# Delta-rule stage of a four-layer decoder: the triangular inverses of two steps in flight, their rounds issued in pairs, the inverse put together by ScalarE

## The reference, cut to what matters

```python
mixed = silu(causal_conv4(x @ Wqkv.T));  q, k, v = split(mixed)
z, b, a = x @ Wz.T, x @ Wb.T, x @ Wa.T
beta = sigmoid(b);  g = -exp(A_log) * softplus(a + dt_bias)
q, k = l2norm(q) / sqrt(128), l2norm(k)
for t in range(64):
    state = state * exp(g[t])
    delta = (v[t] - state.T @ k[t]) * beta[t]
    state = state + outer(k[t], delta)
    out[t] = state.T @ q[t]
y = (rmsnorm(out) * norm_w * silu(z)) @ Wout.T
```

## Time and profile before

| | |
|---|---|
| runs of before | 4779.5, 4787.9, 4791.57 us; median 4787.9 us |
| profiled execution: its span, the only time given for it | 4786.8 us |
| PE, DVE, ACT, POOL busy over the span | 86%, 68%, 44%, 32% |
| projection 0 of step 0 starts | at 2238.71 us of the span |
| last residual addition of the stage ends | at 4132.07 us of the span |

### The profile page before, as it was taken

How to read it: one execution, slowest core, us unless ns; L and a number is a source line. 1 busy time by engine, 2 the same in 40 slices (tenths; PEclk the granted TensorE clock), 3 DMA queues, 4 the chain that set the end, 5 groups by cost and what they waited for, 6 DMA issues and landing times. The chain is left out here.

```text
span 4786.8 us, 142961 instructions
## 1 busy us (share of the span) xinstructions
PE 4133.9 (86%) x62052; PEld 2708.2 (57%) x62052; DVE 3251.6 (68%) x6025; ACT 2096.0 (44%) x3703; POOL 1514.4 (32%) x1605
## 2 busy tenths in 40 slices
PE   7627886677767887997999999999999999789999
PEld 6415654323325664444677777777777777455555
DVE  7897745788897886754677777777777777531111
ACT  3446533544444554323555555555555555221111
POOL 1001200298893220000443334433344433112222
PEclk9869997888898998998999999999999999789999
DMA  1000000133341001001000000000010000041111
GB/s 34 19 27 11 2 12 20 67 121 119 120 141 37 2 2 34 20 1 40 15 21 21 21 24 21 21 21 21 21 26 23 21 17 4 8 128 53 49 53 44
DMA packets 72967, 175.11 MB, mean 37 GB/s; under 512 B 14578, under 2 KB 27892, under 8 KB 69748
## 3 DMA queue, kind: packets, MB, share of 16 engines
q1 hardware_dynamic: 72340, 165.96, 11.1%
HBM read 163.04 MB, written 2.88 MB: 35 GB/s over the span
## 5 line engine op out<-in xcount | busy, mean ns | idle before, releaser
L1721 POOL TENSOR_TENSOR ssm_ub<-ssm_dtu,ssm_bcn 128x512 f32<-128x512 f32 x256 | 324.4, 1293 | 299.5 <-DMA ssm_bcn<-ssm_bct 297.1
L2485 POOL TENSOR_TENSOR dn_eb<-dn_ee,dn_cc 128x512 f32<-128x512 f32 x64 | 66.7, 1042 | 1034.2 <-DVE dn_cc L2599 1034.2
L3030 DVE TENSOR_TENSOR moe_hh<-moe_si,moe_pu 128x512 f32<-128x512 f32 x104 | 71.4, 688 | 450.5 <-PE moe_pu L2919 444.3
L2527 DVE SCALAR_TENSOR_TENSOR core_XN<-dn_bA,dn_w,core_XN 128x504 f32<-128x504 f32 (+2 forms) x384 | 280.6, 731 | 24.9 <-ACT core_XN L2361 4.9
L1620 ACT ACTIVATE ssm_da<-core_XN,ssm_al 128x504 f32<-128x504 f32 x240 | 163.2, 683 | 253.5 <-DVE ssm_ph L1788 169.0
L2982 POOL TENSOR_TENSOR moe_hw<-moe_hh,moe_cb 128x512 f32<-128x512 f32 x100 | 126.6, 1266 | 444.2 <-DVE moe_hh L3030 392.7
L2963 ACT ACTIVATE moe_si<-moe_pg 128x512 f32<-128x512 f32 x104 | 62.1, 597 | 467.7 <-PE moe_pg L2919 467.7
L2191 PE MATMUL dn_bA<-core_XT,dn_w 128*128 128x512 f32 x512 | 258.8, 629 | 9.0 <-ACTq L2453 4.4
L1608 PE MATMUL ssm_py<-ssm_hc,core_ident 128*128 128x512 f32 x352 | 200.6, 675 | 61.7 <-DVE ssm_hc L1792 31.2
L2325 PE MATMUL dn_po<-dn_wo,dn_cT 128*128 128x256 f32 x1024 | 242.1, 390 | 2.6 <-issue 1.4
L1788 DVE TENSOR_TENSOR_SCAN ssm_ph<-ssm_da,ssm_ub 128x512 f32<-128x512 f32 x168 | 204.9, 1220 | 29.3 <-POOL ssm_ub L1721 17.1
(11 more groups left out here) (498 smaller groups left out, 10429.9 us busy)
## 6 DMA issues: line engine op xcount, KB each, us to landing
ssm_bcn<-ssm_bct SPq DMA_DIRECT2D x128, 512.0 KB, 3.6
dn_cb<-dn_cum SPq DMA_DIRECT2D x32, 512.0 KB, 5.0
dn_w<-in_dn_w SPq DMA_DIRECT2D x32, 388.0 KB, 3.3
moe_cb<-moe_rows SPq DMA_DIRECT2D x64, 192.0 KB, 2.8
moe_w<-in_moe_w SPq DMA_DIRECT2D x26, 384.0 KB, 7.5
moe_cb<-moe_rows SPq DMA_DIRECT2D x64, 128.0 KB, 3.0
dn_wo<-in_dn_w SPq DMA_DIRECT2D x16, 256.0 KB, 5.2
moe_cb<-moe_rows SPq DMA_DIRECT2D x64, 64.0 KB, 2.6
```

The lines of the kernel that those rows point to most:

```text
L1721: pool.tensor_tensor(ub[u % NUB][:, :], dtu[q % 2][:, c, :], bcn[i % NB][:, 0, :], ALU.mult).then_inc(ub_ready, 1)
L2527: last = dve.scalar_tensor_tensor(dst[:, :, n:S], src[:, :, 0:S - n], w[i // NCH % 2][:, at:at + 1], dst[:, :, n:S], ALU.mult, ALU.add)
```

## The change

The inverse of a step now takes two passes of the loop. In pass i the rounds 1 and 2 and `level_z` of round 3 belong to step i-1 (**mid**), the rest of round 3 and the rounds 4 and 5 to step i-2 (**late**), and the old group is that of step i-3. PE issues a `level_z` of one step and a `level_x` of the other directly behind each other: z1 with x3, z4 with x1, z2 with x4, z5 with x2, z3 with x5. The five pairs stand where PE's new order has them: XF products; pair 1; projection 1; values products; pair 2; projections 2 and 3; pair 3; gate 0; key products; pair 4; gate 1; turning; values 0; query norms; pair 5; values 1; output weights; turning of the norms; projection 0 of the next step. The loop has one pass more.

`zz` is double, `PT`, `vv`, `rb` and `sk` threefold. The XF products go into `po` (so they wait for the residual addition, `y_added`), and `Mt`, `cn`, `cT` are in order of the value head. The query norms use `bB`, values 0 `bA`, values 1 `bC`. `XF` is written by ACT: `diagonal` after round 4, `corner` after round 5. POOL waits for `corner` (`xf_ready`) before it writes the new `XB`, and signals the first `mb` by itself. DVE's convolution 3 stands behind the key norms.

The loop, and PE:

```diff
-            for i in range(NSTEP + 2):
+            for i in range(NSTEP + 3):
...
+                def first(i):
+                    if i % NCH == 0:
+                        take(pe, w_loaded[i // NCH % 2], 32)
+                    project(i, 0, bA)
...
-                    new, mid, old = i < NSTEP, 0 < i <= NSTEP, i >= 2
+                    new, mid, late, old = i < NSTEP, 0 < i <= NSTEP, 1 < i <= NSTEP + 1, i >= 3
+                    even, odd = zz[i % 2], zz[(i + 1) % 2]
...
+                        take(pe, xf_ready)
+                        take(pe, y_added)
...
+                    if late:
+                        take(pe, zz_ready)
+                    if mid:
+                        level_z(i - 1, 1)
+                    if late:
+                        level_x(i - 2, 3, even)
                     if new:
+                        if i:
+                            take(pe, tq_done)
                         project(i, 1, bB)
...
+                    if mid:
+                        take(pe, zz_ready)
+                    if late:
+                        level_z(i - 2, 4)
+                    if mid:
+                        level_x(i - 1, 1, odd)
+                    if new:
+                        if i:
+                            take(pe, vv_done)
                         project(i, 2, bC)
...
                         take(pe, raw_free)
                         project(i, 3, bA)
+                    if late:
+                        take(pe, zz_ready)
                     if mid:
-                        level_x(m, 2)
+                        level_z(i - 1, 2)
+                    if late:
+                        level_x(i - 2, 4, even)
                     if new:
                         gate(i, 0, bB)
...
+                    if mid:
+                        take(pe, zz_ready)
+                    if late:
+                        level_z(i - 2, 5)
+                    if mid:
+                        level_x(i - 1, 2, odd)
+                    if new:
+                        gate(i, 1, bC)
...
+                    if new:
                         take(pe, raw_free)
+                        take(pe, silu_ready)
+                        values(0, bA)
+                        take(pe, sq_ready)
+                        take(pe, zs_done)
...
+                    if late:
+                        take(pe, zz_ready)
                     if mid:
-                        level_z(m, 4)
+                        level_z(i - 1, 3)
+                    if late:
+                        level_x(i - 2, 5, even)
+                    if new:
+                        take(pe, silu_ready)
+                        take(pe, zs_done)
+                        values(1, bC)
...
+                        pe.transpose(bB[:, P:2 * P], sqr[:, :], g.ident[:, :]).then_inc(sst_ready, 1)
+                    if i + 1 < NSTEP:
+                        take(pe, vv_done)
+                        first(i + 1)
```

ACT:

```diff
+                def diagonal(m):
+                    take(act, diag_ready)
+                    x = halves(XB[m % 2][:, 1, :])
+                    act.activation(XF[:, :, 0:HB], x, ACT.Copy)
+                    act.activation(XF[:, :, HB:S], x, ACT.Copy, scale=second_half)
+
+                def corner():
+                    take(act, p5_ready)
+                    act.drain()
+                    for b in range(BPT):
+                        low = slice(b * S + HB, (b + 1) * S)
+                        last = act.activation(XF[low, :, 0:HB], halves(pm[low, 1, 0:NS * HB]), ACT.Copy)
+                    last.then_inc(xf_ready, 1)
...
+                def roots(i):
+                    take(act, ssk_ready)
+                    act.activation(lk[:, :], ssk[i % 2][:, :], ACT.Ln)
+                    act.drain()
+                    act.activation(sk[i % 3][:, 0, :], lk[:, :], ACT.Exp, scale=0.5)
+                    for b in range(BPT):
+                        act.activation(sk[i % 3][rowsof(b), 1, :], lk[rowsof(b), :], ACT.Exp, scale=0.5)
...
                         silu(0)
                         silu(1)
+                        tap(i, 3, bA)
+                    if mid:
+                        copy_z(odd)
...
+                    if late:
+                        diagonal(i - 2)
+                        copy_z(even, -1.0)
...
+                    if late:
+                        corner()
+                    if new:
+                        values(i, 0, bA)
+                        values(i, 1, bC)
+                        roots(i)
```

POOL:

```diff
+                    if i >= 2:
+                        take(pool, xf_ready)
+                    pool.tensor_tensor(halves(XB[i % 2][:, 0, :]), b0[:, :, :], bcm(small[:, 0, :], NS), ALU.add).then_inc(xt_ready, 1)
+                    for l in range(1, NL - 1):
+                        last = pool.tensor_tensor(halves(mb[i % 2][:, l - 1, :]), BD[:, :, :], bcm(small[:, 1 + l, :], NS), ALU.mult)
+                        if l == 1:
+                            last.then_inc(mb1_ready, 1)
+                    last.then_inc(mb_ready, 1)
```

DVE, in `update`:

```diff
-                    dve.drain()
-                    dve.tensor_copy(XF[:, :, 0:HB], halves(x[:, 1, :]))
-                    dve.tensor_scalar(XF[:, :, HB:S], halves(x[:, 1, :]), second_half, None, ALU.mult)
-                    take(dve, px_ready)
-                    dve.drain()
-                    for b in range(BPT):
-                        low = slice(b * S + HB, (b + 1) * S)
-                        last = dve.tensor_copy(XF[low, :, 0:HB], halves(pm[low, 1, 0:NS * HB]))
-                    last.then_inc(upd_ready, 1)
```

DVE, in `step`:

```diff
                         conv(i, 0, bA)
+                    if late:
+                        update(i - 2, 3)
+                    if new:
                         conv(i, 1, bB)
                     if mid:
-                        update(m, 1)
+                        update(i - 1, 1)
...
                         conv(i, 2, bC)
-                    if mid:
-                        update(m, 2)
+                    if late:
+                        update(i - 2, 4)
...
-                    if new:
-                        conv(i, 3, bA)
...
+                        conv(i, 3, bA)
+                    if mid:
+                        update(i - 1, 2)
+                    if new:
                         take(dve, eb_ready)
...
+                    if new:
+                        take(dve, sst_ready)
+                        dve.tensor_scalar(rb[i % 3][:, :], bB[:, P:2 * P:32], 1e-6, 128e-6, ALU.add, ALU.mult).then_inc(tq_done, 1)
```

More of the change, by code:

```diff
@@ L2037, in l3_attn @@
         BD = s.sb("BD", [P, NS, HB])
[L2038 to L2039 removed]
+        PT = [s.sb(f"PT{k}", [P, NS, S]) for k in range(3)]
+        vv = [s.sb(f"vv{k}", [P, NS, P]) for k in range(3)]
         cs = s.sb("cs", [P, NT, H])
@@ L2056, in l3_attn @@
         cT = s.sb("cT", [P, NS, P])
-        zz = s.sb("zz", [P, NS * HB])
+        zz = [s.sb(f"zz{k}", [P, NS * HB]) for k in range(2)]
         Mt = s.sb("Mt", [P, NS, S])
@@ L2473, in step @@
                 def step(i):
-                    new, old = i < NSTEP, i >= 2
-                    o = i - 2
-                    if new:
-                        take(pool, ee_ready)
-                        if i + 2 < NSTEP:
-                            decays(i + 2)
-                    if i % NCH == 1 and new:
+                    if i >= NSTEP:
+                        return
+                    take(pool, ee_ready)
+                    if i + 2 < NSTEP:
+                        decays(i + 2)
@@ L2573, in step @@
                         conv(i, 2, bC)
-                    if mid:
-                        update(m, 2)
+                    if late:
+                        update(i - 2, 4)
                     if old:
                         take(dve, f_ready)
-                        for n in range(NS):
-                            last = dve.scalar_tensor_tensor(cn[:, n, :], heads(po[:, :, :])[:, n, :], fo[:, n:n + 1],
-                                                            heads(zs[o % 4][:, :, :])[:, n, :], ALU.mult, ALU.mult)
+                        for h in range(2):
+                            for j in range(TPC):
+                                n = h * TPC + j
+                                last = dve.scalar_tensor_tensor(cn[:, n, :], heads(po[:, :, :])[:, n, :], fo[:, n:n + 1],
+                                                                heads(zs[o % 4][:, :, :])[:, 2 * j + h, :], ALU.mult, ALU.mult)
                         last.then_inc(cn_ready, 1)
-                    if new:
-                        conv(i, 3, bA)
                     if i == 0:
                         dve.reciprocal(bt[:, :, :], bt[:, :, :])
-                    if mid:
-                        update(m, 3)
                     kq = bD[:, :].rearrange("p (j w t) -> p j w t", w=2, t=S)
```

221 lines of the change are left out of this document (93 added, 128 removed).

## The result

The changed kernel takes 4808.8 us (median of 5 runs, 4799.9 to 4815.7) against 4787.9 before (5 runs on the same chip): ratio 1.0047, 95% interval 1.0033 to 1.0062. It is slower by 0.5%; 4737 us and a gain of 1.1% were forecast, and 4809 lies above the range. The profiled execution's span is 4813.9 us, 27.1 more than before.

A forecast was written before the change was run, and what follows sets the result against it. PE's list of pieces was taken to bound the stage. Period 28.61 - 0.80 - 0.20 - 0.17 + 0.30 = 27.74 us; over 61 passes -53, first passes -14, end +16: -51, giving 4737 us, range 4708 to 4770.

The forecast's parts named there:

- PE's pieces and their edges: PE's list of pieces laid end to end, with 0.20 us lost per full-array run touching small tiles: 27.74 us a pass.
- edges and pairs: On PE, four fewer runs of full-array pieces save 0.80 us a pass, five pairs for ten rounds 0.20.
- The wait ahead of values 0: New wait of PE for DVE's convolution 3 to leave `bA`: 0.2 to 0.4 us a pass, taken as 0.30.
- The first passes: Stage start, up to step 3's XF products: lighter because the old group enters later, -14 us (bounds -6 and -20).
- the end: Stage end: a third pass without new work, +16 us (bounds +10 and +23).
- XF by ACT: DVE's four copies move to ACT, about 2 us a pass there with two roots: nothing of the sum directly.
- the one on the pairs: Small instructions on PE in five pairs, not ten rounds: five edges of 0.04, 0.20 us a pass saved; products unchanged.
- the four cases: The forecast of 4737 us (chance 0.57) and The three rivals.
- The three rivals: Dearer PE edges, 4712 us (0.20); DVE's chain taking PE's place, 4771 (0.14); the way over `corner`, 4826 (0.09).
- the way over `corner`: ACT's `corner` late, delaying POOL's `XB`, DVE's transposition, residual addition and XF products: slower, 4826 us, chance 0.09.

The follow-up runs named there:

- the kernel with DVE's new order alone: The changed kernel, unpadded, with DVE's convolution 3 ahead of the key norms' reciprocal and factors, and `XB` turned last: 4787.8 us, 1.0014 of before.

## Why the prediction was wrong

**Right.** PE's pieces and their edges: an undisturbed pass takes 27.55 us, 27.74 was forecast. A pair holds PE 1.24 us (32.67 - 31.43 and 37.54 - 36.30 in the trace), not the 1.32 of two rounds, which is more than the whole difference. Projections 2 and 3 together take 36.30 - 32.67 = 3.63 (3.64 forecast), though they start 34.49 - 32.67 = 1.82 apart and not 1.7. Joining the pairs saves 28.40 - 27.55 = 0.85 us against the kernel with them apart, which has hardly any wait at values 0; with that wait added, 1.16, where 1.00 was counted for edges and pairs. The wait ahead of values 0, where and how long. The first passes (-19.7 for -14) and the end (+14.6 for +16). XF by ACT: nothing. The XF products waited for the residual addition only at the end of the stage, 1.3 to 1.4 us ahead of the last three.

**Wrong.** The step is the one on the pairs: "The same number of small instructions in five pairs rather than ten rounds: five edges of 0.04, 0.20 us. The products themselves stay." They do stay, but PE does not get them at that rate. The whole reckoning laid pieces end to end and let only other engines make PE wait; "PE is busy for 398.4 of 400 us" was read as proof that nothing else limits it. It only said that nothing did at 128 small instructions in a row. The page of before had 490 packets on the instruction queue, and its trace 1468 PE instructions a pass, and both would have asked the question; none of the four cases had the instructions' supply in it. What took its place, in 61 passes: 61 x 27.55 = 1681 us undisturbed, 64 less than before; 64.5 us of gaps put to "issue"; ten stretches at 1.2 GHz, about 16; 1.3 for the residual addition. The 13 that are left of the 1775.9 are nearly all the gaps' own: the view counts idle time from the modelled end of the last small matmul, 0.19 us after its start, where the next one otherwise starts 0.01 after it. From start to start the same breaks add up to 77.6 us.

The three rivals did not come about either. The nearest in size, "the way over `corner`" with 4826, has the right sign by a mechanism that did not occur: PE never waits for ACT's inverse.

**Open.** What delays a packet beyond the usual 0.9 us behind its limit, and why PE needs 2.5 us from a packet's start where the packet itself takes 0.9 to 1.5. How many microseconds of the gaps would stay if the packets came sooner wasn't tried.

## What to carry to other kernels

Count instructions as well as work. Where an engine takes many instructions of a few nanoseconds in a row, look for idle time put to "issue" inside a group that waits for nothing, and see whether the gaps share a remainder by 256. A long run of tiny matmuls is best broken by something long: in the two kernels with rounds of 128 instructions and long pieces between them, 3 and 9 us of gaps were left in the full passes. If it can't be broken, the place of the limits matters, and a pass padded to a whole number of blocks can be quicker than a shorter one, at the price that any later edit moves them. Joining pieces saves their edges only as long as the joint run can be supplied.

## What the runs showed of the hardware

PE's instructions come in blocks of 256 (64 bytes each), one packet a block, and where PE had to stop at a limit it went on 2.2 to 3.0 us after the start of the packet that belongs to the limit before. With the median of 0.9 us from a limit to its packet that makes about 3.4 us a block, 13 ns an instruction (an estimate from these two), where 32 x 32 matmuls and their weight loads use up 5. It is not a floor: 465 of the 4328 blocks went by in under 3.3 us and the quickest in 1.7, its packet having started 1.2 us ahead of the limit. A gap is 0.2 to 2 us, at most 2.5 (the kernel with doubled rounds). Kernels whose full passes are alike to the instruction differ by 0.8% and 1.3% through the offset alone. And of the 21 idle times of 1.35 us or more in 61 passes of the changed kernel ten were followed by 3.4 us at 1.2 GHz, though PE was busy nearly all the time on both sides. In the kernel with DVE's new order alone one such fall came behind 1.17 us.
